# A small GpSimd write, and a wait for it, between the indirect DMAs of a routed expert kernel

## The reference

```python
x = x + 0.5 * _L0_ffn_ref(_layernorm(x, axis=-1), L0_ffn_Wg, L0_ffn_Wup, L0_ffn_bup, L0_ffn_Wdown, L0_ffn_bdown)
x = x + _L0_attn_ref(_layernorm(x, axis=-1), L0_attn_Wg, L0_attn_bg, ...)
x = x + 0.5 * _L0_ffn_ref(_layernorm(x, axis=-1), L0_ffn_Wg, L0_ffn_Wup, L0_ffn_bup, L0_ffn_Wdown, L0_ffn_bdown)
```

## Time and profile before

| what | value |
|---|---|
| median of three runs | 853.14 us (850.62, 853.14, 855.24) |
| the profiled execution, its own time | 848.97 us |
| its span, first to last instruction | 846.9 us |
| PE, ACT, DVE, POOL busy | 76%, 61%, 44%, 49% of the span |
| mean busy share of the DMA engines in the span's middle | 1 to 4 tenths |
| granted TensorE clock, mean | 0.873 |

### The profile page before, as it was taken

One profiled execution on the slowest core, in us unless ns is written; L12 is line 12 of the kernel. 1 busy time (PEld: TensorE's weight loads), 2 busy tenths in 40 slices (PEclk: granted clock), 3 DMA queues, 4 the chain that ended last, 5 costly groups with the idle time before them and its releaser, 6 DMA issues. The chain is left out here.

```text
span 846.9 us, 17502 instructions
## 1 busy us (share of the span) xinstructions
PE 639.4 (76%) x4525; PEld 580.4 (69%) x4525; DVE 375.0 (44%) x1735; ACT 514.1 (61%) x1465; POOL 414.2 (49%) x424
## 2 busy tenths in 40 slices
PE   7678669788877789876762888955847778898896
PEld 5467569687867677765661777844746668888894
DVE  8654756320102467754351447844441552222224
ACT  4474545676755588763641678934634656667685
POOL 1444364566555461334446665135344655666552
PEclk9998788899986899967885799968757999999999
DMA  9941312223423232111221322211113332132243
GB/s 244 248 141 44 98 59 58 76 78 110 126 72 88 54 91 60 47 36 60 76 79 46 91 78 79 60 51 40 39 46 90 87 105 64 52 96 74 62 174 100
DMA packets 98984, 71.50 MB, mean 84 GB/s; under 512 B 13504, under 2 KB 91894, under 8 KB 98890
## 3 DMA queue, kind: packets, MB, share of 16 engines
q1 hardware_dynamic: 82890, 42.84, 18.4%
q0 software_dynamic: 13024, 26.11, 10.8%
q10 hardware_dynamic: 2976, 1.44, 0.6%
HBM read 36.30 MB, written 34.75 MB: 84 GB/s over the span
## 5 line engine op out<-in xcount | busy, mean ns | idle before, releaser
L1213 ACT ACTIVATE hT<-ps,BU 128x128 f32<-128x128 f32 x900 | 259.8, 388 | 202.1 <-remote 92.5
L1026 PE MATMUL ps<-xT,WT 128*128 128x128 f32 x1800 | 274.9, 300 | 69.5 <-issue 34.1
L1039 PE MATMUL ps<-WD,hT 128*128 x1800 | 274.3, 298 | 59.2 <-issue 42.1
L1026 PEld LDWEIGHTS ps<-xT,WT 128*128 128x128 f32 x1800 | 249.6, 213 | 85.9 <-issue 84.0
L1039 PEld LDWEIGHTS ps<-WD,hT 128*128 128x128 f32 x1800 | 247.9, 212 | 71.3 <-issue 70.9
L2066 DVE TENSOR_TENSOR Ys<-ps,BD 128x128 f32<-128x128 f32 x225 | 64.0, 288 | 374.0 <-PE ps L1039 209.8
L806 POOL DMA_INDIRECT xs<-XN,SX x144 | 145.2, 1008 | 171.2 <-issue 110.6
L824 POOL DMA_INDIRECT YG<-ys,SY x132 | 134.9, 1022 | 85.8 <-issue 45.3
L1092 ACT ACTIVATE WT<-WU 128x512 f32 x225 | 149.6, 666 | 8.1 <-PE ps L1026 2.9
L836 POOL DMA_INDIRECT yk<-Ys,row x71 | 70.8, 997 | 63.8 <-DVE Ys L2066 37.9
L1186 ACT ACTIVATE xT<-ps 128x512 f32<-128x512 f32 (+1 forms) x52 | 31.8, 611 | 45.4 <-remote 38.2
(11 more groups left out here) (369 smaller groups left out, 604.0 us busy)
## 6 DMA issues: line engine op xcount, KB each, us to landing
ys<-Ys SPq DMA_DIRECT2D x41, 256.0 KB
xl<-xs SPq DMA_DIRECT2D x94, 64.0 KB
xl<-xs SPq DMA_DIRECT2D x71, 66.0 KB
WU<-in_L_ffn_Wup_dram SPq DMA_DIRECT2D x12, 256.0 KB, 5.0
WD<-in_L_ffn_Wdown_dram SPq DMA_DIRECT2D x12, 256.0 KB
YG<-yk SPq DMA_DIRECT2D x4, 768.0 KB, 6.0
xs<-XN,SX POOLq DMA_INDIRECT x144
YG<-ys,SY POOLq DMA_INDIRECT x132
```

The costliest lines, as they stand in the source:

```text
L1026: x = e.matmul(HB[i % 2][:, c * P:(c + 1) * P], WT[i % NW][:, c, :], xT[m % 2][:, j * P:(j + 1) * P], start=True, stop=True)
L1039: x = e.matmul(YB[i % 2][:, 0:D], hT[i % 3][:, c * P:(c + 1) * P], WDf[:, bass.ds(r + c * P, P)], start=(c == 0), stop=(c == C - 1))
L1213: x = e.activation(hT[i % 3][:, c * P:(c + 1) * P], HB[i % 2][:, c * P:(c + 1) * P], ACT.Gelu, bias=BU[:, bass.ds(b + c, 1)])
```

## The change

A tile `idle` (128 partitions of 32 bf16 elements) and a semaphore `s_idle` are added. Behind each of the 407 indirect DMAs POOL writes zeros into `idle` and raises the semaphore. In front of each indirect DMA but the first, `keep_pace` waits until the write that follows the DMA before it is done. Nobody reads `idle`. The order of the DMAs and all other waits stay.

```diff
@@ -430,6 +430,7 @@
         pad = sb("pad", [P, DXW])
+        idle = sb("idle", [P, 32], BF16)
@@ -496,7 +497,7 @@
-        s_xp0, s_xh0 = sem("s_xp0"), sem("s_xh0")
+        s_xp0, s_xh0, s_idle = sem("s_xp0"), sem("s_xh0"), sem("s_idle")
@@ -771,6 +772,8 @@
             def keep_pace(j):
 
+                if j:
+                    e.wait_ge(s_idle, j)
                 if j % K == 0 and tiles_by(j) > 0:
                     e.wait_ge(s_up, tiles_by(j))
@@ -792,6 +795,7 @@
                 e.indirect_dma_start(
                     xl[m % NXL][:, k % 4, 0:D], None, xna if k < NA[0] else xnb if k < NM else xnc, bass.IndirectOffsetOnAxis(SG[:, k:k + 1], 0),
                     bounds_check=a_top if k < NM else x_top, oob_is_err=False).then_inc(s_air[j % AIR], 16)
+                e.memset(idle[:], 0.0).then_inc(s_idle, 1)
...
```

## The result

The changed kernel takes 829.83 us (median of 4 runs, 826.21 to 834.86) against 854.17 us before (850.62 to 855.24): 0.9726 of it, 95% interval 0.9657 to 0.9795. It is faster by 24 us; I had forecast 50. The profiled execution took 834.86 us, the slowest of the four; its span is 833.1 us, 13.8 us under the 846.9 us of before, so the traces account for rather more than half of the difference of the medians.

What follows compares the result with a forecast made beforehand. PE and ACT bound the kernel, held up by long runs of indirect DMAs on POOL. From the 853.14 us median, 87 us of loss less 32, 0.5 and some 4 gives 50 off: 803 us, 8-in-10 range 775 to 868.

Steps and rivals of the forecast that it cites:

- The rival that nothing is eased: Whole kernel: stalls stay, only 0.5 us at the end and perhaps a few waits added; 848 to 857 us, chance 0.17.
- The write, 0.13 us: On POOL behind each of 407 indirect DMAs: the 128x32 bf16 write takes 0.13 us.
- The wait, 0.12 us: On POOL, from the end of a write to the start of the instruction waiting for it: 0.12 us.
- the write and its wait come in series, the gap stands once: Between POOL's DMAs: 0.13 + 0.12 = 0.25 us added to the 0.30 us idle; starts 1.55 us apart, not 1.30.
- The rival that the gap swallows it: Between POOL's DMAs: write and wait fit into the 0.30 us idle, spacing stays 1.30 us; 853 us, chance 0.05.
- The balance at 1.47 to 1.63 us: In POOL's runs: DMA spacing at which no backlog builds up, from 1 to 2 us of recovery after six DMAs.
- the term of 87 us of loss: Long POOL runs: PE and ACT lose 68.5 to 105.3 us there, middle 87 us, before the change.
- the ten stretches: Parts of the span holding POOL's long runs, 183.70 us and 129 DMAs: PE busy 53%, ACT 31%.
- the undisturbed case: Six stretches with no run over 6 DMAs, 258.10 us: PE busy 85.1%, ACT 73.2%, taken as the full rate.
- The 32 us that I took off for longer runs on POOL: Long runs: 129 DMAs x 0.25 us make POOL 32 us longer, subtracted from the gain.
- The end, 0.5 us: Behind the last tile: the last two DMAs each add 0.25 us, uncovered, 0.5 us in all.
- the rival in which POOL becomes the bound: Last phase, 107 DMAs: above 1.66 us per DMA POOL sets the pace, stalls staying; 858 to 892 us, chance 0.18.

Runs made afterwards that it cites:

- the table: Changed kernel, wait first, 0 (before), 1, 2, 3, 4, 6 writes behind all DMAs: 854, 831.5, 809.4, 746.9, 726.4, 751.4 us.
- the plain DMAs: Kernel before, with the 48 gathers of phase 1's results replaced by plain POOL DMAs of the same size: 820.49 us, ratio 0.9618.
- the kernel with two tiles: Changed kernel with two scratch tiles in turn, each DMA waiting only for the write ahead of the DMA before it: 862.14 us, ratio 1.013.
- with the wait first: Changed kernel with the wait on s_idle moved to be the first wait of each of the four DMA functions: 831.51 us, ratio 0.9746.
- with four writes: Changed kernel with four writes of 128x24 behind all 407 DMAs and the s_idle wait ahead of other waits: 726.37 us, ratio 0.8545.

## Why the prediction came out as it did

**What bounds the kernel: right, and larger than I took it for.** Runs of indirect DMAs hold PE, ACT and DVE up, and the spacing decides how far: the table shows it, and the plain DMAs show that POOL's indirect ones are the cause. The rival that nothing is eased is refuted. ACT was busy 23% beside the indirect DMAs and 91% beside plain ones. The rule of the Trainium skill (SBUF — State Buffer, SBUF: two separate sides) by which it would have held, that TensorE and ScalarE never wait on anyone, is about ports of SBUF, and no run here shows that the stalls go through these; as a forecast of the time it was wrong.

**The write, 0.13 us: right** (0.14 to 0.15). **The wait, 0.12 us: right as what it adds** (0.11 by the kernel with two tiles). Taken as I had taken it, from the end of a write to the start of what waits for it, it is 0.28 us, and the gap is in it.

**Where the prediction failed: "the write and its wait come in series, the gap stands once", 0.25 us.** The gap of 0.30 us isn't a cost that stands beside the write. The write runs inside it (1.29 us with the write alone), and only the wait of 0.11 us is new: 1.40 us instead of 1.55. The rival that the gap swallows it was right for the write and wrong for the wait; I had bounded the two together, at 0 and 0.73 us, and put the value too high between. This decides the time: with the wait first, and so about 1.41 us everywhere and no 0.78 or 0.85 us anywhere, the kernel takes 831.51 us, no better than the changed one. So 0.11 us of spacing are worth some 23 us; the 50 had been forecast for 0.25 us.

**The balance at 1.47 to 1.63 us: right, in part by luck.** I had divided a recovery of 1 to 2 us by six DMAs. The trace before, counted from the end of POOL's last DMA to the next work of PE and ACT, shows 1.2 to 1.4 us after the run of 12 of the earlier trace rows, 2.0 to 2.2 us after a run of 15 (from 240.16 us) and 2.6 us (ACT) to 4.4 us (full groups of PE's loads) after the run of 21. By the same division that is 1.40 to 1.51 us, mostly below where the time falls; what happens between two DMAs is not shown by it. At 1.40 us, below the balance, the stalls shrink and stay: ACT 43% in the long runs, and 34 us gained up to DMA 300. From 1.48 to 1.57 us the time falls by 83 us, and at 1.57 us ACT is busy 75 to 77% in the windows shown, above the 73% of the earlier trace rows. At the spacing that I had forecast, 1.55 us, the time would have been between 727 and 747 us by the table (with the wait first), not 803: the term of 87 us of loss, taken from the ten stretches, was too small. The two errors, of the spacing and of the loss, partly cancel, and without that the forecast would have been further off. It left out the short runs of up to 6, which I had used as the undisturbed case (with four writes DMA 0 to 88 take 153.4 us instead of 169.2 and the last phase 169.6 instead of 176.8), and the clock, whose mean was lower beside the stalls (0.873, and 0.933 with four writes): PE's work itself took 41 us less there. The 32 us that I took off for longer runs on POOL were not to be seen up to 1.57 us; no run shows them apart.

**The end, 0.5 us: wrong.** The idle time behind the write is 0.85 us where another wait is written ahead of this one, and `scatter_y` is such a place. The last phase then goes by 1.97 us per DMA and takes 21.7 us longer. This is the rival in which POOL becomes the bound, with the threshold that I gave (1.66 us per DMA), confined to the last phase: 107 x 1.97 = 211 us against 198.5 measured. It came true beside the forecast and not in its place, and took 21.7 of the 34 us off again that had been gained up to DMA 300. Of those 34 us, 12.2 were gained up to DMA 88, where the same late place of the wait made the spacing wide ahead of the gathers; so over the whole kernel the place of the wait changed next to nothing.

**What stays open.** Why starts of indirect DMAs some 1.5 us apart are far enough, and by what way closer ones reach PE, ACT and DVE at once, no run shows. It isn't the bytes, nor chiefly the rows, nor POOL's being busy (49% of the span before, 74% with four writes, where the stalls are all but gone).

## What to carry to other kernels

Where several engines slow down together and nobody they wait for can be named, lay the timeline of the engine that issues indirect DMAs beside them, and change the spacing of its DMAs in small steps: here 0.27 us between two of them were worth 128 us, and 0.06 us more cost 25. Cost a small instruction not by its own length but by what it does to the gap in which it stands, and cost a wait by its place in the list of waits. And cut the span at a few fixed instructions before summing up: a gain of 34 us and a loss of 22 can look like one small gain.

## What was not expected of the hardware

- A semaphore wait that is the first of those in front of an indirect DMA costs 0.11 us, one that stands behind another wait 0.5 to 0.6 us more: the idle time in front of the DMA is 0.28 us in the one case and 0.78 to 0.85 us in the other, and writing the wait first makes it 0.28 us everywhere.
- Small writes that follow each other on POOL overlap: one of 128x32 lasts 0.14 us, but each further one adds 0.06 us, one of 128x16 0.04 us, and one of 128x6 or 128x8 some 0.03 us.
- An indirect DMA of 64 rows keeps POOL busy for 0.94 us, one of 128 rows for 0.98 to 1.00; a plain DMA of 128 rows of 512 bytes takes POOL 0.53 us.
- A last indirect DMA once kept POOL for 5.37 us instead of 0.98, at the very end of the kernel with the wait first.
